# Metaformer block (conv-style triangle product and mixture of experts) on one core: TensorE's unit of the last stage in seven stretches of one tile shape

## What is computed

```python
a = ln_in(_ln_c(x))
left  = mask * (a @ Wl + bl) * sigmoid(a @ Wlg + blg)
right = mask * (a @ Wr + br) * sigmoid(a @ Wrg + brg)
t = einsum('bikc,bjkc->bijc', left, right)
x = x + (ln_c(t) @ Wo + bo) * sigmoid(a @ Wg + bg)
tok = x.reshape(tokens, 64)
z = ln_t(tok)
p = softmax(z @ Wr8 + b8)                  # 8 experts
top_p, top_i = top_k(p, 2); top_p /= sum(top_p)
out = tok + sum_k top_p[k] * (z @ We[top_i[k]] + be[top_i[k]])
```

## Time and profile before

| | |
|---|---|
| time, median of 3 runs | 1067.54 us (1066.48 to 1073.78) |
| the profiled execution | 1074.22 us |
| its span, first to last instruction | 1072.4 us |
| TensorE busy, share of the span | 94% |
| VectorE | 80% |
| GpSimd | 58% |
| ScalarE | 42% |

### The profile page before, as it was taken

How to read it: one execution, slowest core, us unless ns; L and a number is a source line. 1 busy time by engine, 2 the same in 40 slices (tenths; PEclk the granted TensorE clock), 3 DMA queues, 4 the chain that set the end, 5 groups by cost and what they waited for, 6 DMA issues and landing times.

```text
span 1072.4 us, 18725 instructions
## 1 busy us (share of the span) xinstructions
PE 1007.5 (94%) x5688; PEld 558.3 (52%) x5688; DVE 856.0 (80%) x2961; ACT 452.0 (42%) x810; POOL 626.3 (58%) x603
## 2 busy tenths in 40 slices
PE   4798999979999689999999999999999999999996
PEld 3566666758886444444444444444444444444432
DVE  4899999931224589899989998999899999999883
ACT  1455566611111134444444444444444444444432
POOL 5997888432221246656665666566656665666543
PEclk9999999989999679999999999999999999999999
DMA  7678768989991123233333333333333332333231
GB/s 184 197 260 280 283 240 256 344 265 280 290 288 33 50 60 107 91 103 95 104 94 97 101 100 98 92 106 95 102 91 107 92 106 90 109 90 107 78 80 59
DMA packets 119381, 152.93 MB, mean 143 GB/s; under 512 B 10486, under 2 KB 76278, under 8 KB 117238
## 3 DMA queue, kind: packets, MB, share of 16 engines
q1 hardware_dynamic: 118150, 151.32, 47.1%
q10 hardware_dynamic: 1136, 0.46, 0.2%
HBM read 67.33 MB, written 50.33 MB: 110 GB/s over the span
## 4 chain that ended last, share of the span: by engine, by line
PE 80%; DVE 11%; POOL 4%; DMA 2%; issue 1%; ACT 1%; SPq 0%; DVEq 0%; POOLq 0%
PE b_m L794 24%; PE ring L781 10%; PE ein L692 9%; PE b_d L742 7%; PE b_g L732 6%; DVE stage L871 6%; PE pr_a L655 5%; PE b_g L719 3%; PE ring L802 3%; DVE bst L858 3%; PE b_m L788 3%; PE b_t L719 3%; PE b_g L725 3%; PE ring L809 2%; DMA chunk<-left_right_scratch 2%; PE xt_a L643 1%
## 5 line engine op out<-in xcount | busy, mean ns | idle before, releaser
L459 POOL TENSOR_TENSOR zb<-bcs,x2d 128x512 f32<-128x512 f32 x224 | 286.1, 1277 | 267.8 <-ACT bcs L572 267.8
L794 PE MATMUL b_m<-zb,w_exp 128*64 128x512 f32 x1024 | 277.4, 620 | 2.2 <-DVE zb L1032 1.4
L1032 DVE TENSOR_TENSOR zb<-ring,x2d 128x512 f32<-128x512 f32 x288 | 197.7, 687 | 58.1 <-PE ring L781 51.1
L572 ACT ACTIVATE bcs<-ring 128x512 f32<-128x512 f32 x224 | 133.8, 597 | 206.5 <-PE ring L781 206.5
L871 DVE SCALAR_TENSOR_TENSOR stage<-pr_a,mt,sig_a 128x128 f32<-128x128 f32 x512 | 147.8, 418 | 12.0 <-ACT sig_a L518 11.8
L655 PE MATMUL pr_a<-w_proj,xts 64*128 64x256 f32 x1024 | 139.2, 402 | 13.8 <-DVE stage L871 13.4
L781 PEld LDWEIGHTS ring<-wt,sel 64*128 64x128 f32 x512 | 48.0, 184 | 169.4 <-DVE zb L1032 80.7
L781 PE MATMUL ring<-wt,sel 64*128 64x512 f32 x512 | 128.1, 497 | 3.1 <-DVE zb L1032 2.3
L655 PEld LDWEIGHTS pr_a<-w_proj,xts 64*128 64x128 f32 x1024 | 96.0, 190 | 42.4 <-issue 21.6
L451 POOL TENSOR_TENSOR tn<-t_all,rr 128x512 f32<-128x512 f32 x64 | 87.3, 1363 | 36.9 <-DVE rr L960 23.2
L518 ACT ACTIVATE sig_a<-pr_a 128x512 f32<-128x512 f32 x128 | 76.5, 598 | 71.4 <-PE pr_a L655 71.3
(11 more groups left out here) (132 smaller groups left out, 1529.6 us busy)
## 6 DMA issues: line engine op xcount, KB each, us to landing
left_right_scratch<-stage SPq DMA_DIRECT2D x16, 2048.0 KB, 7.7
x2d<-x2t SPq DMA_DIRECT2D x256, 128.0 KB, 2.9
chunk<-left_right_scratch SPq DMA_DIRECT2D x24, 1024.0 KB, 10.8
xc<-in_x SPq DMA_DIRECT2D x64, 256.0 KB, 3.2
out<-outc SPq DMA_DIRECT2D x64, 256.0 KB, 2.0
chunk<-left_right_scratch SPq DMA_DIRECT2D x12, 384.0 KB, 8.3
chunk<-left_right_scratch SPq DMA_DIRECT2D x8, 192.0 KB, 6.1
chunk<-left_right_scratch SPq DMA_DIRECT2D x4, 256.0 KB, 8.4
```

The lines of the kernel that those rows point to most:

```text
L459: pool.tensor_tensor(zb[:, m % NZ, :], bcs[:, tiles_before(POOL_TILES, ku, ku, m) % 2, :], x2d[:, ku % 2, m % 2, :], ALU.mult)\
L572: act.activation(bcs[:, tiles_before(POOL_TILES, ku, ku, m) % 2, :], ring[:, bcast_bank(ku % 2, m), :], ACT.Copy).then_inc(bcast_out, 1)
L794: ins = pe.matmul(b_m[t * C:(t + 1) * C, :], w_exp[:, ep, :], zb[:, (2 * ep + t) % NZ, :], start=False, stop=ep == EP - 1, skip_group_chec ...
L1032: dve.tensor_tensor(zb[:, m % NZ, :], ring[:, bcast_bank(ku % 2, m), :], x2d[:, ku % 2, m % 2, :], ALU.mult)\
```

## The change

TensorE's list of the last stage is put in another order, so that neighbours use the same tile shape (rows x columns of the array): 64 x 128 for bcast(2), bcast(3), back, bcast(4), bcast(5); 128 x 64 for expert 0 and 1; 128 x 128 for x_turn, pack, bias and y_turn; 64 x 128 for bcast(6), bcast(7), turns and the next unit's bcast(0), bcast(1); 128 x 64 for expert 2; 64 x 64 for out_gate; 128 x 64 for expert 3. To fit the shapes, turns transposes each half of 64 rows for itself (16 instead of 8 transposes, the halves into two banks `gt`), and back multiplies each half by a 64 x 72 `route` (a sum of two identities beside the router weights): 8 matmuls of 72 columns instead of 4 of 144, the halves into two banks of b_d. y_turn moves from ring to bank 0 of b_d, pack to bank 1 of gt; ring is left to bcast, bank m % 2. The gating part runs two units further ahead: out_gate for unit u + 6, x_turn for u + 5. GpSimd takes the four odd tiles in every unit. zb has six buffers in turn, x2t seven. On VectorE the slot is ordered anew, with total of a unit at its end.

```diff
-POOL_TILES = [(1, 3, 5), (1, 3, 5, 7)]
+POOL_TILES = (1, 3, 5, 7)
+DVE_TILES = (0, 2, 4, 6)
-NZ = 4
+NZ = 6
+LEAD = 5
-X2 = 6
+X2 = 7
-BACK = P + 2 * E
+BACK = C + E
...
             def turns(n):
...
+                for part, src in enumerate((xn, tn)):
                     for j in range(JP):
-                        m = pe.transpose(dst[:, pairs[j]], src[:, 2 * j:2 * j + 2, :].rearrange("p j c -> p (j c)"), ident)
+                        for r in range(2):
+                            m = turn_half(r, part * N + j * C, src[rows[r], 2 * j:2 * j + 2, :].rearrange("p j c -> p (j c)"))
...
+            def y_turn(u):
+                pe.wait_ge(sum_done, u + 1)
+                pe.wait_ge(back_done, min(u + LEAD + 1, UNITS))
...
+                    m = pe.transpose(b_d[:, 0, pairs[j]], x2t[:, u % X2, pairs[j]], ident)
...
             def back(w):
                 for j in range(JP):
+                    for t in range(2):
+                        m = pe.matmul(b_d[:, t, j * BACK:(j + 1) * BACK], x2t[rows[t], w % X2, pairs[j]], route[rows[t], :],
+                                      start=True, stop=True)
...
             def expert(ep, u):
+                if ep == 0 and u >= 1:
+                    pe.wait_ge(sum_done, u)
```

More of the change, by code:

```diff
@@ L66, with tiles_before, tile_buffer, buffer_used @@
 PARTS = [b + sum(c == b for early in EARLY.values() for c, _, _ in early) for b in range(2)]
[L68 to L94, removed]
+def tiles_before(tiles, u, m=0):
+    return u * len(tiles) + sum(t < m for t in tiles)
+def tile_buffer(u, m):
+    return (u * TILES + m) % NZ
+def buffer_used(u, m):
+    before = u * TILES + m - NZ
+    return before // 2 + 1 if before >= 0 else 0
 def after(n, k):
@@ L604, in _ @@
-            for u in range(-4, UNITS + 1):
-                slot(u, u % (2 * CYCLE) if u >= 0 else u)
+                    bcast(3, u)
+                if has(v):
+                    gate(v)
+                if has(u):
+                    bcast(5, u)
+                if u % 2 == 0 and has(u + 2):
+                    soft((u + 2) // 2)
+                if u % 2 == 1 and has(u + 1):
+                    pack((u + 1) // 2)
+                if has(u):
+                    bcast(7, u)
+                if has(n):
+                    copies(n)
@@ L813, in slot @@
-            def slot(u, ku):
-                if has(u + 3):
-                    back(u + 3, ku + 3)
+            for u in range(-LEAD - 1, UNITS + 1):
+                v, n = u + LEAD, u + LEAD + 1
                 if has(u):
-                    bcast(2, u, ku)
-                    bcast(3, u, ku)
-                if has(u + 4):
-                    turns(u + 4, ku + 4)
+                    bcast(2, u)
+                    bcast(3, u)
+                if has(v - 1):
+                    back(v - 1)
@@ L841, in slot @@
+                if has(n):
+                    turns(n)
                 if has(u + 1):
-                    bcast(0, u + 1, ku + 1)
-                    bcast(1, u + 1, ku + 1)
-            for u in range(-4, UNITS + 1):
-                slot(u, u % (2 * CYCLE) if u >= 0 else u)
+                    bcast(0, u + 1)
+                    bcast(1, u + 1)
+                if has(u):
+                    expert(2, u)
+                if has(n):
+                    out_gate(n)
+                if has(u):
+                    expert(3, u)
@@ L1125, in slot @@
+                bn(3)
                 rstd(7)
[L1126 to L1140 removed]
```

582 lines of the change are left out of this document (264 added, 318 removed).

## The result

The changed kernel takes 1082.49 us (median of 4 runs, 1081.20 to 1083.98) against 1067.53 us: a ratio of 1.0117, 95% interval 1.0092 to 1.0143. It is slower by 15 us, the forecast was 1081. The profiled execution has a span of 1079.4 us, 1072.4 before. Executions of the kernel before, those beside the later runs included, go from 1065 us at a mean granted clock of 0.990 to 1075 us at 0.974, and the profiled one (1074.22 us, 0.976) is of the slow kind, while the four after the change all stand at 0.971 to 0.974.

The account below looks back on a forecast made before the run. The prediction took TensorE's list to bound the last stage before, and a circle of waits through VectorE after. Units +12, fill +8 and end -5 made about +14 us on the 1067.54 median: 1081 us, range 1065 to 1098.

Parts of the forecast that it names:

- The bound before: Last stage, old kernel: the unit is as long as TensorE's list, 10.75 us, with VectorE at 90%.
- The circle: Last stage, once a unit: expert 3, total, scale(2) to scale(6), bcast(0), expert 2, out_gate, expert 3; plus 0.22 us a unit.
- The walk: Priced steps from expert 3 to the next: 11.01 us in even units, 10.91 in odd, mean 10.97 against 10.75.
- TensorE's list: TensorE's own work in a last-stage unit after the change, without waits: 9.7 to 10.2 us.
- A change of shape: TensorE's tile-shape switch: 0.1 to 0.2 us each; five fewer a unit save 0.5 to 1.0 us.
- turns at 0.86: In each unit, TensorE's sixteen half transposes run as eight side-by-side pairs at 0.11 us each, about as before.
- rows 4: Profile rows of stage one's project matmuls, next group 1.93 us after; read as pairs side by side, weight loads hidden under streams.
- The ends: Fill and end of the last stage: fill plus 8 us with slots of 9.1, end minus 5 with units of 8.6.
- The sum: Whole kernel: +12 for 53 full units, fill +8, end -5, about +14 us, giving 1081 us.
- The first: Rival: TensorE's list stays the bound in the last stage; units of 9.7 to 10.2 us, about 1025 us; chance 0.10.
- The second: Rival: row pairs don't run side by side, turns takes 1.71 us; +29 us, 1110 us; chance 0.10.
- The third: Rival: TensorE, waiting 1.2 to 1.5 us a unit, loses its clock; +35, about 1115 us; chance 0.10.

Follow-up runs that it names:

- run 7: Kernel before the change, with VectorE's router operations 1 to 18 and rstd operations 2 to 10 made one-column memsets, reciprocal set to 1: 1057.14 us.
- run 1: Changed kernel with the next unit's bcast(0) and bcast(1) issued behind expert 2 on TensorE instead of ahead of it: 1060.36 us.
- run 2: Changed kernel with scale(6) directly behind residual on VectorE, ahead of the bn_stats, router and rstd operations that stood between: 1073.50 us.
- run 6: Changed kernel with VectorE's router operations 1 to 18 and rstd operations 2 to 10 made one-column memsets, reciprocal set to 1: 1040.32 us.
- run 3: Changed kernel with a unit's total on VectorE moved behind scale(2) of the next unit instead of ahead of it: 1114.74 us.
- run 11: Changed kernel with late bcasts, VectorE reordered and its router and rstd operations memsets; turns transposes all first halves, then all second ones: 1040.32 us.
- run 5: Changed kernel with next-unit bcasts behind expert 2, VectorE's back, logits, residual and scale(6) ahead of most small operations, softmax behind ScalarE's copies: 1036.89 us.

## Why the prediction was right, step by step

**The bound before** stands: run 7 relieves VectorE of a fifth of its work and the unit stays within 0.07 us. **The circle** stands. Run 1 takes TensorE's expert 2 out of it, run 2 seven VectorE operations, run 6 all small operations, and each shortens the unit, while run 3, which removes VectorE's longest wait and not the circle, lengthens it.

**The walk.** Counted from expert 3, the even unit shown above has total at 1.12 (1.13 forecast), scale(2) 1.73 (1.73), scale(4) 3.19 (3.18), the logits copy 6.42 (6.40), residual 6.55 (6.53). y_turn came at 6.74 instead of 6.66. In 25 of the 28 even units scale(6) follows at 7.83 (7.81) and expert 3 at 11.03 (11.01); in the unit shown, one of the three long ones, scale(6) is 0.16 later, for a reason that the trace does not show. The odd unit takes 10.80 (10.91), as scale(6) comes at 7.61 instead of 7.70. The long mean is 10.92 against 10.97. VectorE's waits of 1.3 to 1.7 us, TensorE's 0.85 at y_turn and 0.4 at bcast(0) came as forecast, and so did the 0.3 at bcast(4), which shows there on the weight loads alone. Per unit +0.17, not +0.22: 9 us instead of 12.

**TensorE's list.** A change of shape costs 0.14 us, in the range. The list, 9.91 us with 0.26 of wait in it and an estimated 9.65 without, lies within 9.7 to 10.2 or just below, because one of its terms was mis-sized: turns at 0.86 took 0.59. The price of a whole transpose was taken for a pair of halves; the row of the new order gives 64 columns to each, not 128, and run 11 shows that pairs do run together. back at 0.86 fits: the 1.12 us from its start to bcast(4) hold the wait of 0.26 for scale(2). The 0.27 at turns does not show in the change, which this list does not bound; in a kernel that it bounds it would be 15 us over 58 units.

In the Trainium skill, TensorE: Matmul & The Clock Gate, Part 3, a weight load overlaps a running matmul only where its row group differs. The prediction set rows 4 against this rule, but with 0.9 ns a column, which it had taken from rows 4 itself, so they could not test it. The 1.3 us that it worked out for turns by the rule did not come: with the halves in turn it is 0.59. Run 11 agrees with the rule in so far as turns grows to 0.88 us with neighbours on the same rows. Whether it is the load or the stream that no longer overlaps there, no run here separates.

**The ends.** The fill was mis-sized: from the first turns to the first bcast(2) 44.4 us (342.27 to 386.71) against 39.7, plus 4.7 instead of plus 8, since a slot takes 8.2 to 8.9 us (turns at 348.38, 356.56, 364.85, 373.63) and not 9.1. At the end units 60 to 62 take 8.7 (8.6 forecast). From bcast(2) of unit 0 to the last expert 3 it is 686.99 us against 681.17: +5.8, of which the units are +9 and the end -3, not -5.

**The sum.** From the first turns to the last expert 3 the two traces differ by +10.5 us, where +14 was forecast; as the last stage begins 3.5 us earlier in the trace after (342.27 against 345.78), the spans differ by 7.0. The medians differ by 15.0. That 1081 is so close to 1082.49 is therefore partly luck: the prediction added its +14 to a median 6.7 us below the profiled execution that it had read. In that execution the granted clock is 0.71 from 345 to 370 us and 0.50 from 370 to 385. Executions of the kernel before near its median show 0.986 to 0.988 over the whole, so they ran at the half clock for less time; where, no trace shows. Of the 15 us, then, 9 are the ring of waits, and some 7 go with a clock that the kernel before often kept and the change in none of its four executions; the start (-3.5), the fill (+4.7) and the end (-3) nearly cancel.

**Rivals.** The first (TensorE's list stays the bound) was wrong for this order of VectorE's work and nearly right for another: run 5 comes to 10.11 us a unit and 1037 us, with the list, wait included, at 9.91. The gain in TensorE's list is real, 10.68 to 9.91 us; the other waits take 1.01 us a unit (9.91 to 10.92) where they took 0.07. The second falls for turns. The third did not occur in the change; in run 3 it did.

## What to carry to other kernels

A shorter list on the bounding engine pays only as far as the way through the other engines is shorter than it: walk the ring of waits from one engine's last piece to its next, before the gain is booked. A wait is moved off it by issuing what others wait for first (a bank's last reader, the scale that frees a buffer) and what nobody waits for behind it; run 5 won 46 us with the same instructions. VectorE's longest wait was not the cause but the slack of the ring: removing it alone (run 3) cost 32 us.

## What the runs showed that was not expected

Sixteen transposes of 64 rows, halves in turn, take 0.6 us where eight of 128 take 1.0. A wait can hide on the weight loads: between back and bcast(4) TensorE's matmul rows show almost no gap, and only the load's row names the 0.26 us for scale(2). TensorE's clock can fall inside a stage that is 90% busy: in run 3, with waits of 1.2 us in each second unit, it fell to 0.5 for some us three times between 400 and 1000 us; in the change, with waits of 0.85, it did not. And the fill, at half clock in the profiled execution before, ran at the full one in run 7's (back waited 0.85 us there, 1.51 before): executions of one kernel do either, and between the two medians that goes with some 7 us, nearly as much as the ring.
